# A routed feed-forward stage whose expert rows are added to the output in DRAM, with all shared blocks ahead of the experts

## What is computed

```python
def _L1_ffn_ref(x, gate_w, W1, W2, Ws1, Ws2):      # E = 8, K = 2, H = 192, NS = 2
    xf = x.reshape(-1, D)                          # 4096 tokens of D = 256
    scores = jax.nn.softmax((xf @ gate_w.T), axis=-1)
    top_vals, top_idx = jax.lax.top_k(scores, K)
    w_dense = jnp.zeros((T, E)).at[jnp.arange(T)[:, None], top_idx].set(top_vals)
    y, g = jnp.split(jnp.einsum('td,ehd->teh', xf, W1), 2, axis=-1)
    eo = jnp.einsum('teh,edh->ted', y * jax.nn.silu(g), W2)
    z = jnp.einsum('te,ted->td', w_dense, eo)
    return z + _gated_mlp(xf, Ws1, Ws2)            # the shared expert, hidden width 384
x = x + jnp.tanh(g_ffn[1]) * _L1_ffn_ref(_layernorm(x, axis=-1), ...)
```

## Time and profile before

| what | value |
|---|---|
| median of three runs | 1094.0 us |
| the profiled execution: its time | 1098.07 us |
| the profiled execution: its span, first to last instruction | 1096.3 us |
| mean granted TensorE clock (1 is 2.4 GHz) | 0.944 |
| busy share of the span: PE, DVE, ACT, POOL | 88%, 71%, 53%, 32% |
| DRAM traffic | 38.5 MB read, 57.6 MB written |

### The profile page before, as it was taken

One profiled execution on the slowest core, in us unless ns is written; L12 is line 12 of the kernel. 1 busy time (PEld: TensorE's weight loads), 2 busy tenths in 40 slices (PEclk: granted clock), 3 DMA queues, 4 the chain that ended last, 5 costly groups with the idle time before them and its releaser, 6 DMA issues. The chain is left out here.

```text
span 1096.3 us, 22536 instructions
## 1 busy us (share of the span) xinstructions
PE 962.1 (88%) x6381; PEld 811.3 (74%) x6381; DVE 776.9 (71%) x2237; ACT 575.6 (53%) x1349; POOL 355.6 (32%) x551
## 2 busy tenths in 40 slices
PE   4999999999996679999999999854888889999973
PEld 3667666676764358999999999844777779999862
DVE  3677777777752436888888888855766658888767
ACT  1588888878884423443444434316355266556520
POOL 1011111111110013453444534422776514444410
PEclk9999999999998859999999999986989899999996
DMA  6776758576700400010010100201433214444267
GB/s 164 153 147 146 152 119 161 118 159 139 167 1 23 132 26 25 26 50 25 25 50 25 44 31 25 74 1 48 128 124 102 92 54 125 130 126 127 85 221 239
DMA packets 85873, 104.40 MB, mean 95 GB/s; under 512 B 15070, under 2 KB 75438, under 8 KB 85808
## 3 DMA queue, kind: packets, MB, share of 16 engines
q1 hardware_dynamic: 77616, 81.91, 30.4%
q0 software_dynamic: 7632, 21.05, 5.4%
q10 hardware_dynamic: 560, 0.66, 0.2%
HBM read 38.50 MB, written 57.62 MB: 88 GB/s over the span
## 5 line engine op out<-in xcount | busy, mean ns | idle before, releaser
L1604 POOL DMA_INDIRECT expert_out<-early_weights,aim x71 | 69.9, 985 | 101.6 <-DVE aim L1933 57.7
L1142 ACT ACTIVATE f_hidden<-c_hidden,f_b 128x256 f32<-128x256 f32 x128 | 53.7, 471 | 68.2 <-PE c_hidden L1331 68.2
L1595 POOL DMA_INDIRECT sorted_rows<-m_z,slot_i x64 | 71.8, 1122 | 44.4 <-DVE slot_i L1813 26.6
L1329 PE MATMUL c_mlp<-f_w_hi,f_hidden_hi 128*128 128x256 f32 x256 | 80.7, 315 | 3.6 <-DVE f_hidden_lo L1260 3.6
L1329 PE MATMUL c_hidden<-y2T_hi,f_w_hi 128*128 128x256 f32 x256 | 77.1, 301 | 0.0
L1331 PE MATMUL c_mlp<-f_w_hi,f_hidden_lo 128*128 128x256 f32 x256 | 72.4, 283 | 0.0
L1330 PE MATMUL c_mlp<-f_w_lo,f_hidden_hi 128*128 128x256 f32 x256 | 72.4, 283 | 0.0
L1331 PE MATMUL c_hidden<-y2T_hi,f_w_lo 128*128 128x256 f32 x256 | 72.2, 282 | 0.0
L1330 PE MATMUL c_hidden<-y2T_lo,f_w_hi 128*128 128x256 f32 x256 | 72.2, 282 | 0.0
L748 PE MATMUL ps_probT<-ident,prob 128*77 128x128 f32 x512 | 68.8, 279 | 3.8 <-ACT prob L479 3.3
L596 DVE TENSOR_REDUCE mx<-ps_scores 128x8 f32<-128x616 f32 x64 | 50.9, 796 | 28.0 <-PE ps_scores L682 27.9
(11 more groups left out here) (334 smaller groups left out, 3093.5 us busy)
## 6 DMA issues: line engine op xcount, KB each, us to landing
sorted_rows<-no_row SPq DMA_DIRECT2D x15, 2322.0 KB, 13.4
m_z<-sorted_rows SPq DMA_DIRECT2D x71, 129.0 KB
early_weights<-expert_chunks SPq DMA_DIRECT2D x8, 640.0 KB, 4.2
combT<-combineT_all SPq DMA_DIRECT2D x16, 256.0 KB, 2.3
slT<-slots_all SPq DMA_DIRECT2D x16, 256.0 KB, 2.5
early_weights<-expert_out SPq DMA_DIRECT2D x8, 512.0 KB, 6.3
early_weights<-expert_out POOLq DMA_DIRECT2D x8, 512.0 KB, 6.2
out<-x_all SPq DMA_DIRECT2D x8, 512.0 KB, 3.4
```

The costliest lines, as they stand in the source:

```text
L1142: last = act.activation(hf[:, q % 2, j, :], psH[:, q % 2, j, :], ACT.Relu, bias=fb1[:, c_:c_ + 1])
L1329: pe.matmul(out, lh, rh, start=start, stop=False, skip_group_check=shared)
L1595: pool.indirect_dma_start(out=sorted_rows[:, :], in_=zn[:, s % 3, t, :], in_offset=None, out_offset=bass.IndirectOffsetOnAxis(ap=slot_i[:, ...
L1604: pool.indirect_dma_start(out=expert_out[:, :], in_=xo[:, i % 3, :], in_offset=None, out_offset=bass.IndirectOffsetOnAxis(ap=aim_i[:, i % ...
```

## The change

- No part three. All eight shared blocks run in part one. `expert_out`, `back`, `combine`, `FIRST` and `LAST` are gone.
- The output tensor gets 1024 spare rows ahead of the 4096 real ones; they are cut off on the host. One DMA of 1 MB clears them at the kernel's start.
- After each block's `result`, SP writes X of that block to the output (`base_out`), inside part one.
- Each sorted row carries two weights (`ROW` is 260). They are made per block: `topd` at the end of `top_two`, tanh of an eighth of it on ACT, and `weights`, nine small DVE operations that turn tanh into the exponential, ((1+t)/(1-t))^4, and normalise. The scatter of a block now also waits for `weights`.
- In the expert loop ACT multiplies the result by the row's weight as it copies it, and POOL's indirect DMA adds it to the output row in DRAM (`compute_op=ALU.add`). A row that belongs to no token is aimed at a spare row. `aims` is three small DVE operations, not two.
- Since two additions to one row must not overlap, POOL waits before the addition of tile i: for that of i-3 always, and for those of i-1 and i-2 where the tile's expert differs from its forerunner's. A table of flags from `tile_table` (five more small DVE operations) gives the register value that is added to the semaphore count. The result buffer has 12 places (`XO`), not 3, and 12 tiny DMAs raise its semaphores by 16 once, ahead of the first `rstd` on POOL.
- Part one is written as one list `order` of 38 steps, each with a stage 0 to 3: in turn t every engine runs its steps of the list for block t minus stage.
- The router matmul has 8 columns, not 128, and the ranks stand in the router's PSUM bank.

```diff
+def unrolled(eng, order, steps, n):
+    for t in range(n + max(step[0] for step in order)):
+        for stage, name, *part in order:
+            if name in steps and 0 <= t - stage < n:
+                steps[name](t - stage, *part)
...
+            sp.dma_start(self.out[0:SPARE, :].rearrange("(p r) d -> p r d", p=P), spread(no_row[:, :, 0:D], 1, SPARE // P)).then_inc(rows_cleared.sem, 16)
...
+        AHEAD, ROUTE, SHARED, LATE = range(4)
+        order = [(SHARED, "silu", 1), (LATE, "down", 0), (LATE, "hidden_lo", 1), (SHARED, "hidden_hi", 0),
+                 (SHARED, "up", 1), (ROUTE, "z_hi"), (AHEAD, "later_stats"), (SHARED, "places"),
+                 (LATE, "hidden_lo", 2), (ROUTE, "scatter"), (SHARED, "hidden", 0), (AHEAD, "later_rstd"),
+                 (SHARED, "weights"), (LATE, "table"), (AHEAD, "rows_in"), (LATE, "down", 1), (SHARED, "hidden", 1),
+                 (LATE, "down", 2), (ROUTE, "logits"), (ROUTE, "z_lo"), (SHARED, "up", 2), (SHARED, "silu", 2),
+                 (SHARED, "hidden_lo", 0), (AHEAD, "zf_out", 0), (SHARED, "hidden_hi", 1), (AHEAD, "turn_z", 0),
+                 (ROUTE, "expert_hi"), (LATE, "result"), (ROUTE, "silu", 0), (ROUTE, "tanh"), (ROUTE, "top_two"),
+                 (ROUTE, "up", 0), (SHARED, "hidden_hi", 2), (SHARED, "hidden", 2), (AHEAD, "zf_out", 1),
+                 (LATE, "expert_lo"), (AHEAD, "turn_z", 1), (ROUTE, "ranks")]
...
                 sp.dma_start(self.stage_expert(e), ins["expert_chunks"][:, e]).then_inc(stage_in[e % 2].sem, 16)
+                if e >= 4:
+                    base_out(e - 4)
+            for b in range(NE1 - 4, NBLK):
+                base_out(b)
...
+            for j in range(XO):
+                pool.dma_start(self.begun[j:j + 1, :], halves[0:1, :]).then_inc(xo_out[j].sem, 16)
             rstd(0)
...
             for i in range(XT):
+                if i % 16 == 0:
+                    word = pool.value_load(turns_i[0:1, i // 16:i // 16 + 1], min_val=0, max_val=2 ** 20 - 1)
                 pool.wait_ge(aim_done.sem, i + 1)
                 pool.wait_ge(xo_ev.sem, i + 1)
-                pool.indirect_dma_start(out=expert_out[:, :], in_=xo[:, i % 3, :], in_offset=None,
-                                        out_offset=bass.IndirectOffsetOnAxis(ap=aim_i[:, i % 6:i % 6 + 1], axis=0),
-                                        bounds_check=2 * TOKENS - 1, oob_is_err=False).then_inc(xo_out[i % 3].sem, 16)
+                if i >= 3:
+                    added(pool, i - 3)
+                turn = (word >> (i % 16)) & 16
+                for k in (i - 1, i - 2):
+                    if k >= 0:
+                        pool.wait_ge(xo_out[k % XO].sem, turn + 16 * (k // XO + 1))
+                        alone(pool)
+                pool.indirect_dma_start(out=self.out[:, :], in_=xo[:, i % XO, :], in_offset=None, compute_op=ALU.add,
+                                        out_offset=bass.IndirectOffsetOnAxis(ap=aim_i[:, i % AIMS:i % AIMS + 1], axis=0))\
+                    .then_inc(xo_out[i % XO].sem, 16)
...
             def x_out(i):
                 act.wait_ge(xd_mm.sem, i + 1)
-                act.copy(xo[:, i % 3, :], xY[:, i % 2, 0, :]).then_inc(xo_ev.sem, 1)
+                act.wait_ge(aim_done.sem, i + 1)
+                if i >= XO:
+                    added(act, i - XO)
+                act.mul(xo[:, i % XO, :], xY[:, i % 2, 0, :], weight[:, i % AIMS:i % AIMS + 1]).then_inc(xo_ev.sem, 1)
...
-            for i in range(XT + 2):
-                if i == BT:
-                    act.wait_ge(sent[1].sem, 16 * 2 * BT * 3)
-                    apply(LAST[1], 1).then_inc(zn_done.sem, 1)
```

More of the change, by code:

```diff
@@ L1521, in phase_d @@
-        kept = expert_out.rearrange("(i j p t) d -> p i j (t d)", i=2, j=NBLK, p=P)
+        xo_out = [sig(f"x_added{j}", 1, 16) for j in range(XO)]
+        o_out = sig("m_o_out", 1, 16)
+        CHUNKS = NBLK * SC
+        AHEAD, ROUTE, SHARED, LATE = range(4)
[8 more added lines that the diff above has]
+                 (LATE, "expert_lo"), (AHEAD, "turn_z", 1), (ROUTE, "ranks")]
@@ L1598, in _, with later_rstd @@
-                if s in (0, 2):
-                    rstd(s // 2 + 2)
+                        pool.indirect_dma_start(out=sorted_rows[:, :], in_=zn[:, b % 3, t, :], in_offset=None,
+                                                out_offset=bass.IndirectOffsetOnAxis(ap=slot_i[:, b % 2, i, t:t + 1], axis=0))\
+                            .then_inc(sent[b % 3].sem, 16)
+            def later_rstd(b):
+                if b in (0, 2):
+                    rstd(b // 2 + 2)
+            unrolled(pool, order, dict(scatter=scatter, later_rstd=later_rstd), NBLK)
@@ new lines, in _ @@
+                for k in (i - 1, i - 2):
[5 more added lines that the diff above has]
+                    .then_inc(xo_out[i % XO].sem, 16)
+            for i in range(XT - XO, XT):
+                added(pool, i)
@@ L1898, in _ @@
                 shared_lo(n)
-            z_lo(0)
-            expert_lo(0)
-            for s in range(NBLK + 1):
-                first, *others = units(s)
-                if s < NBLK:
-                    top_two(s)
-                hidden(first)
-                hidden_lo(first)
-                if s < NBLK:
-                    places(s)
-                if s + 1 in FIRST:
-                    z_lo(s + 1)
-                if s in (0, 2):
-                    stats(s + 4)
-                    stats(s + 5)
-                if s == NBLK - 1:
-                    tile_table()
-                for m in others:
-                    hidden(m)
-                    hidden_lo(m)
-                if s + 1 < NE1:
-                    expert_lo(s + 1)
@@ L1921, in _, with later_stats, table_last @@
-            result(len(FIRST) - 1)
+            def later_stats(b):
+                if b in (0, 2):
+                    stats(b + 4)
+                    stats(b + 5)
+            def table_last(b):
+                if b == NBLK - 1:
+                    tile_table()
+            unrolled(dve, order, dict(z_lo=z_lo, top_two=top_two, weights=weights, places=places, hidden=hidden, hidden_lo=hidden_lo,
+                                      result=result, expert_lo=expert_lo, later_stats=later_stats, table=table_last), NBLK)
@@ L2071, in down @@
                 last.then_inc(dn_mm.sem, 1)
[L2073 to L2094 removed]
+            unrolled(pe, order, dict(turn_z=turn_z, logits=logits, ranks=ranks, up=up, down=down), NBLK)
             pe.wait_ge(table.sem, 3)
             pe.wait_ge(wel_done.sem, NE1)
[L2098 removed]
+            pe.wait_ge(res_done.sem, NBLK)
             pe.wait_ge(place_done.sem, 4 * NBLK)
```

335 lines of the change are left out of this document (123 added, 212 removed).

## The result

| what | before | after |
|---|---|---|
| median us of seven runs each | 1094.0 | 1089.1 (1086.7 to 1092.7) |
| ratio to before, 95% interval | | 0.9948 [0.9929, 0.9968] |
| the profiled execution: time, span | 1098.07, 1096.3 | 1092.42, 1090.7 |
| first expert tile on PE | 887.6 | 913.2 |
| last result leaves ACT | 1039.6 | 1067.1 |

A forecast was written before the change was run, and what follows sets the result against it. PE was taken to bound only the expert loop; the closing part was a chain of transfers and sums. Closing -51, loop -0.6, part one +28, clearing +1 gave -23 us: median 1071 us, range 1054 to 1090.

The forecast's parts named there:

- Part one: Stretch with shared blocks and routing: grows by 28 us, first expert tile at 916.
- The loop through the load: Part one, turns 3 to 8: expert load, ACT's rounding, DVE's remainder, then next load; 19.4 us per turn.
- The closing part: Stretch after the expert loop: its transfers and sums go, 56.7 us becomes 5.6, -51 us.
- POOL's pace: Expert loop: POOL needs 0.96 + 0.30 us and at most 0.5 more per addition, 1.8, under the 2.07 pitch.
- The close: Kernel's end: 1 us to close after the 4.6 us wait for the last addition.
- The loop: Expert loop: the layer norm of four tiles leaves it, gaining 0.6 us; added DVE and ACT work fits idle time.
- The start: Stage head: twelve tiny DMAs delay the first `rstd` by 2.3 us; clearing 1 MB costs 1 us.
- A: Expert loop: additions landing later than 6.2 us set the pitch; at 8 us, +43 us, 1114; chance 0.13.
- E: Expert loop: additions take twice a plain scatter, 6.4 us, pitch 2.13, +5 us, 1076; chance 0.12.
- C: Part one: PE's clock falls to 1.2 GHz, turns take 23 us, +18 us, 1089; chance 0.12.
- B: Part one: the load doesn't bind, turns run at PE's 16.1 us, 1054; chance 0.13.
- under 8 us from the last copy to the end: Closing part: a sign listed as showing the forecast right, the time from last result copy to kernel end.

The follow-up runs named there:

- the early remainder: Changed kernel with the expert weights' remainder formed two turns earlier, so its load buffer frees sooner: 1067.1 us (ratio 0.9732), again 1069.7 (0.9768).

## Why the prediction was wrong

- **Part one, right.** +28 forecast, +25.6 measured, first tile at 913.2 for 916. The loop through the load was named and ran at 18.7 us for 19.4. The experiment with the early remainder shows it as the cause: without it the first tile starts 0.3 and 3.7 us later than before the change. The closeness of the mean is in part luck: four turns took 18.1 us, and one, with PE at 1.2 GHz for some 8 us, took 21.4 and made up for half of the difference. Behind the turns two errors offset each other too: the last `expert_lo` ended at 881.5 for 886, and from there it took 31.7 us for 30.
- **The closing part, wrong.** The failed step is the sentence "Where the expert changes (seven times) POOL waits for the newest addition too, some 2 us each; twelve result buffers (25 us of the loop) cover it", priced at nothing. The buffers cover the producers and not POOL. A stop makes POOL wait 3 us, and it came eight times (the change to the empty tiles counts too). My 2 us were about the landing less the pace; but from one issue to the next a stop takes 4.5 to 5.5 us, of which the landing is 3.9, so some 0.7 us or more pass between the landing and the next issue.
- **POOL's pace.** I bounded it at 0.96 + 0.30 and 0.5 for small instructions, 1.8, and compared it with 2.07 only to ask whether it is below. It is 1.86, because the adding issue takes 1.56 us; the eight small instructions fit in the 0.30. The sum that was missing is one line: 70 x 1.86 + 8 x 3 = 154 us against 144 for the results, so POOL ends at least 10 us late. With my own figures it would not have warned me: 70 x 1.8 + 7 x 2 = 140 against 70 x 2.07 = 145, and nine tiles between changes make up 9 x 0.27 = 2.4 us, more than a stop of 2. At the measured sizes they make up 9 x 0.23 = 2.1 of nearly 3. So the reason given was wrong, and the pace, the length of a stop and their number were each too small.
- **The close.** I took 1 us from the last landing to the end; it was 5.0, of which POOL's drain is 4.5. In the kernel before a drain of POOL is on record too, but beside the last sums and writes, where it cost nothing; without part three it stands in the open:

```profile
L193 POOLq DRAIN  x1: 10411/10411/10411, 1082.8 to 1082.8; - x1
```

- **A term left out.** The text gives the landing of an addition "1 us at the very end", but the sum keeps the plain wait of 4.6 us and has no such term; it measured 0.6.
- **The loop.** -0.6 forecast, +1.9 measured from the first tile on. From the first to the last result it took 144.4 us for 143.6; the rest, 1.1, is ahead of the first result (9.5 us for 8.4), where PE waits 1.5 us for the second load of rows. Why the pitch grew by 0.01 us no run tells.
- **The start.** The clearing cost nothing that shows: POOL's operations at the head of the stage stand at 736.4 us for 737.1 before, so +1 was too much. The twelve small transfers take POOL 6.5 us, and the first `rstd` starts at 743.1, 0.9 us later than before and not 2.3.
- **The rivals.** A named the right side (additions late) by the wrong mechanism: the landing, at 3.9 us, never reached the 6.2 from which it decides; it was the issue that was long. E was right in that an addition costs the DMA engines more, three times a plain write; but the landing was 3.9 us and not 6.4, and it cost nothing that way. C gives the measured time, 1089, but by turns of 23 us; turns were 18.7. Its mechanism did show, in one turn of the five (3.2 us), and again on another chip (21.0 us at 0.76); it is a small part of the sum. B's state (load not binding) is the early remainder's kernel; its turn, 15.5, lies below the 16.1 that I counted for PE.
- The time lies in the range, at its upper end, where C had put the bound: that is luck, since what filled it up is in the main no rival's mechanism. The chance of 0.78 for faster by over 0.5% stood on the closing part (its terms add up to 0.77, less a little). Of the signs listed ahead, the one that caught the error is "under 8 us from the last copy to the end": it was 23.6.

## What to carry to other kernels

A buffer between a producer and a consumer that is slower once its stops are counted hides the consumer's stops from the producer, but not from the end of the kernel. For each engine behind a buffer add up its whole work over the loop, pace times count plus stops times their length, and compare it with the loop's time; what is over comes out behind the last result. And where one step of a turn frees a buffer for a load, look in how many turns that load is next needed: moving the freeing step two turns forward was worth more here than the change itself.

## What the runs showed of the hardware that was not expected

- Issuing an indirect transfer that adds in DRAM takes GpSimd 1.56 us, the same transfer as a plain write 0.96.
- The addition lands in 3.9 us (3.5 to 5.0), the plain write in 2.4 (2.4 to 4.0); the addition takes three times the share of the DMA engines per MB (49.1% for 7.87 MB and 17.8% for 8.52 MB in stretches of 135 us).
- GpSimd's drain at the end of a block took 4.5 us behind such transfers though all had landed, and 7.2 us behind plain writes. Begun before the last addition had landed, it took 8.4 us and ended 3.5 us behind the landing.
- TensorE ran one turn of five at 1.2 GHz for some 8 us after a wait for a load; an equal wait in the turn before it brought no such fall.
